# Keys and values of the grouped-query stage made in a stage of their own at the front, split once and stored

## What is computed

```python
# layer 0: linear attention over x, context; then a mixture of low-rank experts
x = x + tanh(g_xattn[0]) * linear_attention(layernorm(x), ctx, ctx, ...)
x = x + tanh(g_ffn[0]) * lora_moe(layernorm(x), ...)
# layer 1: grouped-query attention, 32 query heads, 8 key/value heads, head size 128
q = rope(layernorm(x) @ Wq); k = rope(ctx @ Wk); v = ctx @ Wv
logits = 30 * tanh(einsum('btkgd,bTkd->bkgtT', q, k) * 0.0884 / 30)
attn = softmax(where(mask, logits, -1e30)) @ v
x = x + tanh(g_xattn[1]) * attn @ Wo
x = x + tanh(g_ffn[1]) * sign_ffn(layernorm(x), ...)
```

## Time and profile before

| | us |
|---|---|
| median of 3 runs | 3255.17 (3253.72 to 3257.74) |
| the profiled execution | 3260.55 |
| its span, first to last instruction | 3258.8 |
| TensorE busy in the span | 3078.9 |
| POOL busy | 1984.4 |
| VectorE busy | 2082.4 |

### The profile page before, as it was taken

How to read it: one execution, slowest core, us unless ns; L and a number is a source line. 1 busy time by engine, 2 the same in 40 slices (tenths; PEclk the granted TensorE clock), 3 DMA queues, 4 the chain that set the end, 5 groups by cost and what they waited for, 6 DMA issues and landing times. The chain is left out here.

```text
span 3258.8 us, 42040 instructions
## 1 busy us (share of the span) xinstructions
PE 3078.9 (94%) x14675; PEld 2481.3 (76%) x14675; DVE 2082.4 (64%) x2601; ACT 1316.5 (40%) x2010; POOL 1984.4 (61%) x1297
## 2 busy tenths in 40 slices
PE   5999999999759999989999989999998999998799
PEld 3787887878547888878888878888887888886677
DVE  4777777777346566666765675566666656764675
ACT  4555555555233343344333433343343334332322
POOL 5454544544256767776776776766767676764343
PEclk8999999999879999999999999999999999999799
DMA  4111111111142222244222143212242312221321
GB/s 131 33 46 65 33 65 53 46 66 39 52 157 71 79 82 90 71 119 145 79 82 97 64 142 122 97 64 97 68 134 87 135 64 97 70 91 64 133 72 52
DMA packets 179697, 273.39 MB, mean 84 GB/s; under 512 B 8537, under 2 KB 109273, under 8 KB 179593
## 3 DMA queue, kind: packets, MB, share of 16 engines
q1 hardware_dynamic: 179592, 272.09, 24.7%
HBM read 238.51 MB, written 33.55 MB: 83 GB/s over the span
## 5 line engine op out<-in xcount | busy, mean ns | idle before, releaser
L1507 DVE RECIPROCAL g_rot_b<-gp_sum 128x512 f32<-128x512 f32 x128 | 429.0, 3351 | 23.2 <-PE gp_sum L1620 23.0
L1573 PE MATMUL gp_p<-g_xn_hi,g_wq_hi 128*128 128x512 f32 x1024 | 399.4, 390 | 10.9 <-POOL g_wq_lo L1209 10.8
L1573 PE MATMUL gp_p<-g_xn_lo,g_wq_hi 128*128 128x512 f32 x1024 | 398.9, 390 | 0.0
L1573 PE MATMUL gp_p<-g_xn_hi,g_wq_lo 128*128 128x512 f32 x1024 | 398.8, 389 | 0.0
L1637 PE MATMUL gp_y<-g_wo_hi,g_at_lo 128*128 128x512 f32 x992 | 387.1, 390 | 0.0
L1637 PE MATMUL gp_y<-g_wo_lo,g_at_hi 128*128 128x512 f32 x992 | 386.6, 390 | 0.0
L1637 PE MATMUL gp_y<-g_wo_hi,g_at_hi 128*128 128x512 f32 x992 | 386.1, 389 | 0.0
L1484 DVE SCALAR_TENSOR_TENSOR g_res<-gp_y,g_tg,g_res 128x512 f32<-128x512 f32 x256 | 188.2, 745 | 248.4 <-PE gp_y L1637 231.1
L1209 POOL TENSOR_TENSOR g_wq_lo<-g_wq_raw,g_wq_hi 128x1024 fp32r<-128x1024 f32 x132 | 323.6, 2466 | 10.9 <-ACT g_wq_hi L1310 10.9
L1464 DVE TENSOR_TENSOR g_q_raw<-gp_p,g_cos_q 128x512 f32<-128x512 f32 x128 | 88.5, 692 | 363.3 <-PE gp_p L1573 213.0
L1209 POOL TENSOR_TENSOR g_at_lo<-g_at_raw,g_at_hi 128x512 fp32r<-128x512 f32 x128 | 182.5, 1426 | 209.6 <-ACT g_at_hi L1310 209.2
(11 more groups left out here) (245 smaller groups left out, 7517.8 us busy)
## 6 DMA issues: line engine op xcount, KB each, us to landing
g_wq_raw<-in_L_Wq SPq DMA_DIRECT2D x64, 1024.0 KB, 7.6
g_wo_raw<-in_L_Wo SPq DMA_DIRECT2D x62, 1024.0 KB, 6.8
g_wkv_raw<-in_L_Wk SPq DMA_DIRECT2D x32, 512.0 KB, 4.6
g_wkv_raw<-in_L_Wv SPq DMA_DIRECT2D x32, 512.0 KB, 3.7
a_x<-in_x SPq DMA_DIRECT2D x16, 512.0 KB, 4.5
a_cc_f<-in_ctx SPq DMA_DIRECT2D x16, 512.0 KB, 5.1
a_cT<-in_ctxT SPq DMA_DIRECT2D x16, 512.0 KB, 3.6
x_after_layer<-a_x SPq DMA_DIRECT2D x16, 512.0 KB, 2.7
```

What stands on the lines that cost most here:

```text
L1507: V.reciprocal(rsum[:, :], p_sum[:, :]).then_inc(rsum_done, 1)
L1573: mm = M(bank[:, :], w[a][:, i, cols], x[b][:, i, :], start=(i == 0 and t == 0), stop=(i == KT - 1 and t == 2))
```

## The change

A new stage, `key_value_stage`, runs first. It holds the whole context split in hi and lo (loaded once, 8 MB), and for each of eight steps j makes four units of values and four of keys. A value unit is 48 matmuls of 256 columns: a pair of heads for two batches, the tokens as weights, so that the value needs no turning. A key unit is 24 matmuls of 512 columns: head j for four batches. It rotates the keys, splits keys and values, and stores both parts in DRAM as `keys_split` and `values_split`, 512 KB for each turn and each of the two.

`gqa_stage` then loads the ready parts of a turn (`load_k`, `load_v`) and no longer holds or splits the context, Wk or Wv. `project` makes the four query heads only. `attend` begins with two output halves in place of one and the transposes; ACT makes two tanh/exp pairs before the first rounding; the value product has a second PSUM bank; the low parts of Wo are made by POOL (pieces 0 and 1) and VectorE (pieces 2 and 3), both after the rotations of heads 1 and 2.

```diff
+def key_value_stage(nc, ctxT, Wk, Wv, cos_t, sin_t, k_out, v_out):
...
+            def store_k(j, g):
+                n = k_count(j, g)
+                sp.wait_ge(k_lo, n)
+                sp.dma_start(k_out[g * NKV + j], k_sb[n % 2][:, :, :].bitcast(F32)).then_inc(k_store[n % 2], 16)
+            def store_v(j, i):
+                n, g, h = v_count(j, i), pair(j, i) // 2, pair(j, i) % 2
+                sp.wait_ge(emptied, made_v(j, i))
+                for w in range(VW):
+                    sp.dma_start(v_out[g * NKV + VW * quarter(j) + w][:, :, h * 2 * HD:(h + 1) * 2 * HD],
+                                 v_sb[n % 2][:, :, w, :].bitcast(F32)).then_inc(v_store[n % 2], 16)
...
+            load_cx(0)
+            load_wv(0)
+            for b in range(1, 4):
+                load_cx(b)
+            load_wk(0)
...
+            for j in range(NKV):
+                for i in range(PER_J):
+                    store_v(j, i)
+                if j % 2 == 1 and j + 1 < NKV:
+                    load_wv(quarter(j + 1))
+                for g in range(NGRP):
+                    store_k(j, g)
+                if j + 1 < NKV:
+                    load_wk(j + 1)
+            for i in range(2):
+                sp.wait_ge(k_store[i], 16 * NKV * NGRP // 2)
...
+            def v_round(j, i):
+                n = v_count(j, i)
+                act.wait_ge(made, made_v(j, i))
+                after(act, v_store[n % 2], 16 * VW * ((n - 1) // 2))
+                A(v_sb[n % 2][:, 0, :, :], by_head(bank(made_v(j, i))[:, :]), ACT.Copy).then_inc(v_hi, 1)
...
+            def v_low(j, i):
+                n = v_count(j, i)
+                dve.wait_ge(v_hi, n)
+                t = v_sb[n % 2]
+                V.tensor_tensor(t[:, 1, :, :], by_head(bank(made_v(j, i))[:, :]), t[:, 0, :, :].bitcast(F32),
+                                ALU.subtract).then_inc(emptied, 1)
...
+            def finish_k(j, g):
+                n = k_count(j, g)
+                t = k_raw[n % 2][:, 1, :]
+                pool.wait_ge(emptied, made_k(j, g))
+                G.tensor_tensor(t, t, rot[n % 2][:, :], ALU.add).then_inc(rot_done, 1)
+                pool.wait_ge(k_hi, n)
+                G.tensor_tensor(k_sb[n % 2][:, 1, :], t, k_sb[n % 2][:, 0, :].bitcast(F32), ALU.subtract)\
+                    .then_inc(k_lo, 1)
...
+            def value(j, i):
+                u, q = made_v(j, i), quarter(j)
+                after(pe, emptied, u - NPS)
+                out = bank(u)[:, :].rearrange("p (w b n) -> p b w n", w=VW, b=2)
+                for m in range(2):
+                    b = 2 * pair(j, i) + m
+                    if q == 0:
+                        cx_ready(b)
+                    for k in range(KT):
+                        if pair(j, i) == 0 and m == 0 and k % (KT // 2) == 0:
+                            pe.wait_ge(wv_lo, wv_count(q, 2 * k // KT))
+                        for t, (x, w) in enumerate(SPLIT):
+                            mm = M(out[:, m, :, :], tokens(b)(cx[x])[:, k, :], by_head(wv[w][:, k, :]),
+                                   start=(k == 0 and t == 0), stop=(k == KT - 1 and t == 2))
+                mm.then_inc(made, 1)
+            def key(j, g):
+                u = made_k(j, g)
+                after(pe, emptied, u - NPS)
+                if g == 0:
+                    pe.wait_ge(wk_lo, j + 1)
+                if j == 0:
+                    for b in range(NB * g, NB * g + NB):
+                        cx_ready(b)
+                for k in range(KT):
+                    for t, (w, x) in enumerate(SPLIT):
+                        mm = M(bank(u)[:, :], wk[w][:, k, :], cx[x][:, g, k, :],
+                               start=(k == 0 and t == 0), stop=(k == KT - 1 and t == 2))
+                mm.then_inc(made, 1)
...
+            for j in range(NKV):
+                for i in range(PER_J):
+                    value(j, i)
+                for g in range(NGRP):
+                    key(j, g)
...
-            def load_wkv(src, j):
-                sp.dma_start(wkv["raw"][:, :, :], one(src, j)).then_inc(wkv_land, 16)
+            def load_k(n):
+                sp.dma_start(k_sb[:, :, :].bitcast(F32), one(k_in, n)).then_inc(k_land, 16)
+            def load_v(n):
+                sp.dma_start(v_sb[:, :, :].bitcast(F32), one(v_in, n)).then_inc(v_land, 16)
             for dst, src in ((cos_k, cos_t), (sin_k, sin_t), (m8, mask), (tg, gate)):
...
-                    if z.group_end:
-                        load_acts("cx", cx, ctxT, z.g + 1)
-                        load_halves("wq", wq, one(Wq_v, z.j_next))
+                    load_halves("wq", wq, one(Wq_v, z.j_next))
+                    sp.wait_ge(s_done, FIRST + n * NB + NB)
+                    load_k(n + 1)
                 if z.group_start:
...
-                    sp.wait_ge(qk_proj, FIRST + (n + 1) * NR + 1)
-                    load_wkv(Wv_v, z.j_next)
...
                 attn_split(3)
                 if not z.last:
                     for i in range(NR):
                         rotated(n + 1, i)
-                        if i < 4:
-                            wo_split(n, i, wo)
+                        if 1 <= i < 3:
+                            wo_split(n, i - 1, wo)
...
                 softmax(0)
-                act.wait_ge(v_hi, FIRST + 2 * n + 1)
-                round_hi(v, lambda t: t[:, :]).then_inc(v_hi, 1)
+                softmax(1)
                 softmax_hi(0)
-                softmax(1)
                 softmax_hi(1)
...
-                    value_out(n + 1)
+                        if i == 0:
+                            quarters("wo", wo, n + 1, wo_hi, range(4))
...
+            def wo_split(n, m, buf):
+                dve.wait_ge(wo_hi, FIRST + n * 4 + m + 1)
+                subtract_hi(V, buf, part("wo", m // 2, m % 2)).then_inc(wo_lo_dve, 1)
...
+            for i in range(2, 4):
+                dve.wait_ge(xn_hi, FIRST + i + 1)
+                subtract_hi(V, xn, part("xn", i // 2, i % 2)).then_inc(xn_lo_dve, 1)
...
-                        if i == 2:
-                            wkv_split(2 * n + 4)
+                        if 1 <= i < 3:
+                            wo_split(n, i + 1, wo)
...
                 for h in range(G):
-                    if h >= 1:
-                        pe.wait_ge(rot_mul, FIRST + n * NR + h)
-                    projection(p_proj[(h + 1) % 2], wq, slice(h * HD, (h + 1) * HD), xn, n if h == 0 else None)\
-                        .then_inc(qk_proj, 1)
-                pe.wait_ge(wkv_lo, FIRST + 2 * n + 2)
-                pe.wait_ge(rot_mul, FIRST + n * NR + G)
-                projection(p_proj[1], wkv, slice(0, HD), cx).then_inc(v_proj, 1)
...
+                    if h == 1:
+                        pe.wait_ge(attn_done, FIRST + n * NB)
+                    pe.wait_ge(rot_mul, FIRST + n * NR + max(h - 1, 0))
+                    projection(p_proj[h % 2], wq, slice(h * HD, (h + 1) * HD), xn, n if h == 0 else None)\
+                        .then_inc(q_proj, 1)
...
+                    pe.wait_ge(k_land, 16 * n + 16)
...
+                pe.wait_ge(rsum_done, FIRST + n * NB + b)
...
+                if b == 0:
+                    pe.wait_ge(v_land, 16 * n + 16)
+                pe.wait_ge(attn_done, FIRST + n * NB + max(b - 1, 0))
...
+                for h in heads_:
                     if u == 0:
-                        pe.wait_ge(wo_lo, FIRST + n * 4 + h + 1)
+                        if h < 2:
+                            pe.wait_ge(wo_lo, FIRST + n * 2 + h + 1)
+                        else:
+                            pe.wait_ge(wo_lo_dve, FIRST + n * 2 + h - 1)
...
                 out(0)
-                turn_value(n)
+                out(1)
                 scores(n, 0)
...
+            pe.wait_ge(xn_lo, FIRST + 2)
+            pe.wait_ge(xn_lo_dve, 2)
...
-    spent = linear_attention_moe_stage(nc, a["x"], a["ctx"], a["ctxT"], a["L0_WqT"], a["L0_WkT"], a["L0_Wv"], a["L0_WoT"], a["L0_bo"],
+    k_split, v_split = scratch("keys_split", (32, P, 2, BANK)), scratch("values_split", (32, P, 2, BANK))
+    spent = key_value_stage(nc, a["ctxT"], a["L1_Wk"], a["L1_Wv"], a["cos"], a["sin"], k_split, v_split)
+    spent = linear_attention_moe_stage(nc, spent, a["x"], a["ctx"], a["ctxT"], a["L0_WqT"], a["L0_WkT"], a["L0_Wv"], a["L0_WoT"], a["L0_bo"],
...
-    gqa_stage(nc, x2, xnT, a["ctxT"], a["mask"], a["gate_x1"], a["L1_Wq"], a["L1_Wk"], a["L1_Wv"], a["L1_Wo"],
+    gqa_stage(nc, x2, xnT, k_split, v_split, a["mask"], a["gate_x1"], a["L1_Wq"], a["L1_Wo"],
```

More of the change, by code:

```diff
@@ L1048, in gqa_stage @@
         p_s = [ps("s0"), ps("s1")]
-        p_pv, p_sum = ps("pv"), ps("sum")
+        p_pv, p_sum = [ps("pv"), p_proj[1]], ps("sum")
         p_y = [ps("y0"), ps("y1")]
@@ L1285, in body @@
                 if z.last:
-                    for m in range(4):
+                    for m in range(2):
                         wo_split(n, m, wo_last)
@@ L1376, in body @@
                 softmax(2)
-                if not z.last:
```

(2 more changed lines are left out.)

385 lines of the change are left out of this document (253 added, 132 removed).

## The result

The changed kernel takes 3448.25 us (median of 4 runs, 3446.46 to 3449.58), the kernel before, beside it on the same chip, 3256.45 (3253.72 to 3260.86): a ratio of 1.0587, 95% interval 1.0569 to 1.0606. It is 5.9% slower; the prediction said 4.9% (3414 us, range 3315 to 3475). The profiled execution lasts 3447.87 us, its span 3446.1.

A forecast was written before the change was run, and what follows sets the result against it. TensorE's stream of matmuls was taken to bound the kernel. Span 3258.8 + 373 (new stage) - 214.5 (thirty turns 175.5, group ends 8, first head group 31) = 3417.3 us, so 3414 us measured, 4.9% slower; range 3315 to 3475.

The forecast's parts named there:

- new stage: Front stage making all keys and values: 351 us of matmuls plus start, half clock, end and hand-over, 373 us added.
- head of the stage saves: Start of the grouped-query stage: queries go first, and the first head group's attention and projections finish 31 us sooner.
- wait for the second g_wo_lo: Each turn, second head of the first output half: TensorE waits 3.7 us (3.2 to 4.2) for POOL's second Wo low part.
- clock behind it: After that wait the granted clock may fall to half in some turns: 1.6 us a turn, between 0 and 2.85.
- rest of the turn: A loop turn without the wait for POOL and its clock loss: 52.0 us, against 63.15 before.
- what the group end adds to eight turns: At group ends TensorE waits for the query weights' low parts: 9 us plus 1 for the clock, against 12.6 before.
- last head group: End of the loop, costed as even: one more wait for POOL, but two of the last weight parts moved to VectorE.
- rival B: Dearer: value matmuls at 0.147 us (3463), or waits of 4.2 us with the clock falling every time (3466); chance 0.15.
- rival A: Wait for POOL near its floor, clock holding: 3366 us with the wait at 3.7, 3313 at 1.95; chance 0.27.
- C: Faster: POOL in time with its second Wo part in the loop and also at group ends, 3225 us; chance 0.06.
- D: POOL in time in the loop but not at group ends: 3255 us, no change; chance 0.06.
- a lock for a whole instruction: GpSimd and two-input VectorE instructions hold the shared SBUF ports throughout, so both POOL sums are hit: wait 4.2 us.

The follow-up runs named there:

- first run: The new stage put ahead of the kernel before, which still makes its own keys and values and uses nothing of the stage: 3638.7 us, ratio 1.1164.
- the run with copies: Changed kernel with VectorE's two low parts of Wo per turn made as one-input copies of the rounded part instead of subtractions: 3389.7 us, ratio 1.0398.
- one line: Changed kernel with POOL making its two low parts of Wo after the rotations of heads 0 and 1 instead of 1 and 2: 3298.4 us.
- the last version: Changed kernel with Wo parts spread, ACT's old order, two activation parts early and query weights' parts before attention's (batches 1 to 3) at group ends: 3251.5 us.
- the spread version: Changed kernel with ACT rounding Wo before head 0's rounding, VectorE's two Wo parts after head 0, POOL's after heads 0 and 1: 3280.6 us.

## Right and wrong, by the prediction's steps

| step | forecast | measured |
|---|---|---|
| new stage, from first transfer to next stage's | 373 | 378.5 |
| the same, to the grouped-query stage's transfer | 373 | 379.9 |
| of it: first matmul | 10.5 | 10.33 (9.6 after the first transfer) |
| value matmul, start to start | 0.115 | 0.120 |
| key matmul | 0.227 | 0.227 |
| last matmul to next stage's transfer | 8.8 | 8.9 |
| q0 starts / scores (less 379.9) | 907 / 937.5 | 907.0 / 937.4 |
| head of the stage saves | 31 | 29.5 |
| wait for the second g_wo_lo | 3.7 (3.2 to 4.2) | 4.1 |
| clock behind it | 1.6 (0 to 2.85) | 1.6 |
| rest of the turn | 52.0 | 52.2 |
| a turn | 57.3 | 57.90 |
| a group of eight | 468.4 | 471.0 |
| of it: what the group end adds to eight turns | 10 | 7.8 |
| wait for g_wq_lo there | 9 | 4.6 |
| from the last head group's output product to the end | as before | 5.0 more |

**The mechanism** was right in each of its places: the stage is added whole (first run), the wait falls at the second head of the output product with POOL's second part as its releaser, 31 times, and the loop gives back 5.2 us a turn of the 11 that it could. At the group ends the wait is for g_wq_lo, as forecast. The run with POOL's parts one head earlier shows that this wait and its clock are what the changed kernel lacks: 150 of the 192 us by which it is slower.

**The sizes that were off.** The time, 3448, lies in the whole range but above the forecast's own bracket (3385 to 3445, chance 0.46) and in that of rival B (3445 to 3480, chance 0.15), though B's dear value matmuls (0.147) did not come. The span is 28.8 us above the forecast of 3417.3, and the trace divides it into four stretches.

- The new stage, 5.5: the value matmuls (0.005 us on 1536) cost 7.6 more, the start (9.6 us after the first transfer) and the loss at the half clock (first value step 24.69 against 23.03: 1.7, not 3) 2.1 less. The linear-attention stage behind it, costed as unchanged, took 1.4 more.
- The head of the grouped-query stage, 1.5.
- The thirty turns from the first output product to the last, 15.4. The wait: I took 3.7 between 3.2 and 4.2 and should have taken the upper end, since it was worked out from both sums being held for a whole instruction, and the earlier trace rows already showed a sum of 2.28; 0.4 us on 30 turns is 12 us, the rest of the turn (0.2) 6 more. The first turns, where the clock is down for longer, and a group end of before that was only 11.6 us give some 4 more; the group ends, 7.8 us each and not 10, take 6.6 back. So part of the closeness of the forecast is luck, since errors of opposite sign cancel.
- What follows, 5.0. The last head group was costed as even, but it has the wait too: it is 6.8 us longer, and the last stage 1.8 shorter.

The other 6 us are not in the kernel: I lowered the sum by 3.65 because the median of before lay below its profiled execution, while the median of after stands 2.15 above its profiled span.

**The rival A** (wait near the floor of 1.95, clock holding) is excluded by the two delays of POOL's sums, of 1.05 us each: 4.1 less these is 2.0. With half of them, in the run with copies, the wait was 2.9; no run takes them away and leaves the rest as it is. **B**'s upper wait of 4.2 was true, its clock falling every time too, but at 1.6 and not 2.85. **C** and **D** (POOL in time) are what the edited versions show: 3298 with one line, 3251.5 with all. C's 3225 was not reached. By the trace of the last version, 7 us are lost ahead of the grouped-query stage and 17 in its loop: a turn of 52.25 instead of 52.0, in which a wait of 0.3 for the last head's rotation is left, and group ends of 2.7 where C had none.

**The lock.** The prediction gave two readings of the earlier trace rows, a lock for a whole instruction (4.2) and a slowing of overlapped time (3.2). The trace agrees with the first: 4.1, with sums that end 1.14 and 1.15 us behind VectorE's parts. The copies (the same distances at half the delay) and the spread version (no delay where no VectorE part stands beside the sum) show the same from the other side.

## What to carry to other kernels

Taking work off the engine that sets the pace gains something only if the other engines are in time without it, for that work may have hidden their chains. Before removing a projection, write down when each part that is made meanwhile is asked for and when it is ready, and move those parts first. A low part on VectorE (1.23 us) made a sum on POOL 1.05 us longer, so place such parts where the other engine has no instruction on the path. And count the clock behind a stall in dense work: here it fell behind every one of 3.96 us and behind half of those of 2.6 to 2.9, and two short stalls close together brought it down too.

## What was not expected of the hardware

- A one-input fp32 copy of 128x1024 on VectorE (0.69 us) holds up POOL like a subtraction: the sum beside it took 1.79 us instead of 1.28 and ended 1.15 us behind it.
- The clock's answer to a stall comes in steps: at waits of 2.63 and 2.9 us it fell in 11 and 12 of 24 turns, for 1.6 us or, in 5 of these 23, 2.8 to 2.9; at 3.96 in every turn; at 1.0 in none. Two stalls of 1.96 and 1.48 us, 1.0 us apart, cost 2.7.
- Dense matmuls of 256 columns with their own weight load stand 0.120 us apart, against 0.227 for 512 columns: 5.7% more for the same columns.
